# A graph attention phase whose maxima are dealt out three later: seventeen before the first bend, and each head's spread, turn and division three units on

## The chip, the cores and the metric

The kernel runs on one core of one Trainium2 chip. The metric is the time of one execution in microseconds (us), as the median over runs. PE is the matrix engine TensorE, DVE the vector engine, ACT the scalar engine, POOL GpSimd and SP the engine that here only issues DMAs. Every engine works through its own instructions in order and meets the others at semaphores.

## The reference, cut to what matters

A graph of 1250 nodes and 40000 edges goes through a 12-head graph attention with a residual and a layer norm, and then through three relational graph convolutions and a second norm. The change touches the attention alone:

```python
a1 = jnp.einsum('nhd,hd->nh', ft, attn_l)
a2 = jnp.einsum('nhd,hd->nh', ft, attn_r)
e = jax.nn.leaky_relu(a1[src] + a2[dst], negative_slope=NEG_SLOPE)
m = jax.ops.segment_max(e, dst, num_segments=n)
ee = jnp.exp(e - m[dst])
denom = jax.ops.segment_sum(ee, dst, num_segments=n)
alpha = ee / denom[dst]
agg = jax.ops.segment_sum(alpha[:, :, None] * ft[src], dst, num_segments=n)
```

The kernel does it densely: an earlier phase has counted the edges between every pair of nodes into `csum` (1250 x 1250) and has marked the missing ones in `nbr`.

## The kernel before, in words

The attention phase lies between the counting and the convolutions. Its work is cut into units: head h (of 12) and tile s (of 10, 125 nodes each), written (h,s) below, 120 in all, `u = 10 h + s`. For one unit:

- `best(u)` on DVE (line 857): the largest `a1` over the neighbours of each node of the tile, read from `a1`, a row of PSUM spread over all partitions.
- `bend_low(u)` on DVE (869, "bend" below): the first half of the leaky relu, from `r1` (PSUM, the head's lower row spread over all partitions) and `lowb` (SBUF, brought by DMA), into one of five buffers `y`. It waits until POOL has used the buffer: for unit u - 5.
- `bend(u)` and `exponent(u)` on ACT (772, 777): relu, then exponential, the relu of unit u + 1 being issued ahead of the exponential of unit u.
- `weights(u)` on POOL (732): times `csum`, into one of three buffers `pw`. It waits for `gather(u - 3)`.
- `gather(u)` on PE (953): matmuls into the head's sums `po`, in PSUM.

For one head:

- `spread(h)` on PE (919): writes `a1` for the maxima of head h, after all of head h - 1 are taken. Its third piece shares a PSUM bank with `r1`, and waits for a bend.
- `lows(h)` on POOL (705 to 724): eleven small operations that turn the ten maxima of head h into rows; it waits for `maxed` to reach 10 (h + 1), which is all maxima of head h. In POOL's order `lows(h + 2)` stands between `weights(h,9)` and `weights(h+1,0)`.
- `turn_low(h)` on PE (939), then `keep_low(h)` on ACT (782), then DMAs from SP (653, 657, 660) to a row in DRAM and back into `a_rows` and `lowb`.
- `spread_r1(h)` on PE (932): writes `r1` for the bends of head h, issued after `gather(h-1,5)`.
- `keep_sums(h)` on ACT (795), `turn_sums(h)` on PE (961; its result lies where `a1` lies), `divide(h)` on DVE (874 to 879) and `add(h)` on POOL (739) finish the head.

`MAXIMA[s]` lists which tiles of head h + 2 have their maximum taken after the bend of unit (h,s). All twenty maxima of heads 0 and 1 are taken ahead of the first bend. `keep_sums(h-1)` and `keep_low(h+1)` come on ACT after `exponent(h,2)`, and `gather(h,0)` waits for both.

Of the kernel before, what the change touches and what calls it, by code (L numbers as in the profile page):

```python
# [23 lines left out]
T = 125  # L24
NT = N // T
# [554 lines left out]
Y_AT = [(u + 3) % YS for u in range(NU)]  # L580
WIDENED = [6, 7, 8, 9, 0, 1, 2, 3, 4, 5]
GONE = 1e25
MAXIMA = [(), (), (0,), (1,), (2,), (3,), (4, 5), (6,), (7,), (8, 9)]
SPANS = [(0, 512), (512, 512), (1024, N - 1024)]
R1_SPANS = [(286, 512), (798, N - 798), (0, 286)]

# [1 line left out]
def attention(nc, io, dram, stage, x, res, share, oT, cols, csum, csum16, nbr, y, stored, proj_out, rows_out, node, ident):  # L588
# [3 lines left out]
    with ExitStack() as ctx:  # L592
# [99 lines left out]
        def _(pool):  # L692
# [56 lines left out]
                pool.wait_ge(kinds, 4)  # L749

            lows(0)
            lows(1)
            for u in range(NU):
                h, s = divmod(u, NT)
                weights(u)
                if s == NT - 1 and h + 2 < H:
                    lows(h + 2)
                if s == 3 and h >= 2:
                    add(h - 2)
                if s == 5 and h == H - 2:  # L760
                    kinds_and_zeros()
# [5 lines left out]
        @block.scalar  # L767
        def _(act):
            def bend(u):
                h, s = divmod(u, NT)  # L770
                act.wait_ge(zed, u + 1)
                nc.scalar.activation(y[:, Y_AT[u]], y[:, Y_AT[u]], ACT.Relu, scale=-1.0,
                                     bias=a1_low[:, s, h:h + 1]).then_inc(bent, 1)

            def exponent(u):
                act.wait_ge(bent, u + 1)
                nc.scalar.activation(y[:, Y_AT[u]], y[:, Y_AT[u]], ACT.Exp, scale=-1.0).then_inc(raised, 1)

            def keep_low(h):
                act.wait_ge(low_turned, h + 1)  # L780
                act.wait_ge(low_out, 16 * h)
                nc.scalar.copy(row[:], turned_low).then_inc(low_kept, 1)

            def first_low():
                act.wait_ge(low_kept, 1)
                act.dma_start(dram["low"][0].rearrange("m (t p) -> (m t) p", p=T), row[:]).then_inc(low_out, 16)
                act.wait_ge(low_out, 16)
                act.dma_start(a_rows[rows_of(0), :], dram["low"][0, 0:2]).then_inc(r1_in[0], 16)
                act.dma_start(lowb[:, 0], dram["low"][0, 2:3].to_broadcast([T, N])).then_inc(low_in[0], 16)

            def keep_sums(h):
                act.wait_ge(summed, (h + 1) * NT)
                act.wait_ge(low_turned, min(h + 3, H))
                act.wait_ge(o_turned, h)
                nc.scalar.copy(oT, po[:, 0:N].rearrange("p (t n) -> p t n", t=NT)).then_inc(o_kept, 1)

            act.wait_ge(proj_out, 16 * NT)
            for t in WIDENED:
                if t == 0:
                    keep_low(0)  # L800
                    first_low()
                    act.wait_ge(stored[0], 16 * (R + 1) * (NT // 2))
                if t == 3:
                    act.wait_ge(stored[1], 16 * (R + 1) * (NT // 2))
                nc.scalar.copy(csum[:, t], csum16[:, t]).then_inc(widened, 1)
            keep_low(1)
            bend(0)
            for u in range(NU):
                h, s = divmod(u, NT)
                if u + 1 < NU:  # L810
                    bend(u + 1)
                exponent(u)
                if s == 2 and h:
                    keep_sums(h - 1)
                    if h + 1 < H:
                        keep_low(h + 1)
            keep_sums(H - 1)

        @block.vector
        def _(dve):  # L820
# [61 lines left out]
            for t in range(NT):  # L882
                best(t)
            for t in range(NT):
                best(NT + t)
                if t == NT // 2:
                    weight_turned()
            for h in range(H):
                for s in range(NT):
                    bend_low(h * NT + s)  # L890
                    if h >= 2 and s == 1:
                        divide(h - 2)
                    if h == H - 1 and s == 3:
                        degrees()
                    if h + 2 < H:
                        for t in MAXIMA[s]:
                            best((h + 2) * NT + t)
            kind_tables()
            most()
            divide(H - 2)  # L900
# [6 lines left out]
        def _(pe):  # L907
            def spread(h):
                to = a1 if h else r1
                if h >= 2:  # L910
                    pe.wait_ge(maxed, h * NT)
                for i, (o, w) in enumerate(SPANS if h else R1_SPANS):
                    if h == 1 and i == 2:
                        pe.wait_ge(maxed, NT)
                    if h >= 2 and i == 2:
                        pe.wait_ge(zed, (h - 2) * NT + 3)
                    if h >= 4 and i == 0:
                        pe.wait_ge(shared, h - 3)
                    ins = nc.tensor.matmul(to[:, o:o + w], pick[0:A1_K, h:h + 1].to_broadcast([A1_K, T]),  # L919
                                           a_rows[0:A1_K, o:o + w].bitcast(F32R), start=True, stop=True)  # L920
                ins.then_inc(a1_set, 1)

            def spread_r1(h):
# [4 lines left out]
                    pe.wait_ge(maxed, NT)  # L928
                for o, w in R1_SPANS:
                    if o == 0:  # L930
                        pe.wait_ge(maxed, min(h + 2, H) * NT)
                    ins = nc.tensor.matmul(r1[:, o:o + w], pick[at, H:H + 1].to_broadcast([2, T]),
                                           a_rows[at, o:o + w].bitcast(F32R), start=True, stop=True)
                ins.then_inc(r1_set, 1)

            def turn_low(h):
                pe.wait_ge(low_ready, 3 * h + 3)
                pe.wait_ge(low_kept, h)
                nc.tensor.transpose(turned_low, lows_of[:, h % 2].rearrange("p m t -> p (m t)"), ident[0:T, 0:T]).then_inc(low_turned, 1)

            def gather(u):
                h, s = divmod(u, NT)
                pe.wait_ge(weighed, u + 1)
                if s == 0:
# [1 line left out]
                    if h == 0:  # L946
                        pe.wait_ge(ones, 1)
                    pe.wait_ge(o_kept, h)
                    pe.wait_ge(low_kept, min(h + 2, H))
                    if h == 0:  # L950
                        pe.wait_ge(wfc_kept, 2)
                for o, w in SPANS:
                    ins = nc.tensor.matmul(po[:, o:o + w], x[:, s, h], pw[:, u % 3, o:o + w], start=s == 0, stop=s == NT - 1)  # L953
                ins.then_inc(summed, 1)
# [14 lines left out]
            spread(1)  # L969
            turn_low(0)  # L970
            spread_r1(0)
            turn_low(1)
            spread(2)
            for u in range(NU):
                h, s = divmod(u, NT)
                gather(u)
                if s == 5 and h + 1 < H:
                    spread_r1(h + 1)
                    if h >= 1:
                        turn_sums(h - 1)  # L980
                if s == 6 and h + 3 < H:
                    spread(h + 3)
                if s == NT - 1 and h + 2 < H:
                    turn_low(h + 2)
                if s == 5 and h == H - 1:
                    turn_sums(h - 1)
            turn_sums(H - 1)


# [647 lines left out]
```

## Time and profile before

| | |
|---|---|
| median of 3 runs | 2357.75 us (2356.49 to 2358.66) |
| the profiled execution: its time | 2353.26 us |
| its span, first to last instruction | 2351.1 us |
| outside the span | 2.16 us |
| attention phase in the span | 332.8 to 751.4, 418.6 us |
| busy in that phase: PE, DVE, ACT, POOL | 331.0, 369.4, 318.2, 362.2 us |
| mean granted TensorE clock, whole span | 0.969 of full speed |

Times in the profile are microseconds from the start of the span. Over the whole span PE is the busiest engine, but that is the convolutions' doing; the attention phase keeps PE, DVE, ACT and POOL all busy for 76 to 88% of it, and none of them all the time. What sets its length has to be read from who waits for whom in one head.

### The profile page before, as it was taken

What the parts mean: (1) busy time and instruction counts of PE and PEld (TensorE: products, weight loads), DVE (VectorE), ACT (ScalarE), POOL (GpSimd) and SP (SyncE); (2) the same over time, 40 slices, a digit from 0 to 9 for tenths busy, and PEclk for the clock granted to TensorE, in tenths of its full rate; (3) what the DMA queues carried; (4) which work ended last, traced back from release to release, by engine and by line L of the source; (5) the groups of instructions that cost most, each with busy time, mean ns of one, the idle gap of its engine ahead of it and who ended that gap; (6) DMA issues with size and microseconds to landing.
All of it is one profiled execution on the core that took longest, in us unless ns stands there. A gap on an engine that the chain in (4) does not pass through costs nothing.

```text
span 2351.1 us, 29738 instructions
## 1 busy us (share of the span) xinstructions
PE 2151.0 (91%) x10896; PEld 1806.1 (77%) x10897; DVE 1207.6 (51%) x1846; ACT 786.0 (33%) x1071; POOL 515.9 (22%) x565
## 2 busy tenths in 40 slices
PE   4988856888887799999999999999999999999997
PEld 2544532333333799999999999999999899999997
DVE  7887779999977632323323522332322432334335
ACT  1133337888875411212212411211211321212212
POOL 1000016999997100000000100000100100000000
PEclk8999977999998899999999999999999999999998
DMA  1123323111110544334434424333434424345332
GB/s 51 50 93 100 115 94 103 33 34 34 34 36 28 150 136 106 96 87 108 112 90 109 112 73 106 105 96 93 115 98 115 120 71 114 102 115 143 108 93 78
DMA packets 190931, 214.97 MB, mean 91 GB/s; under 512 B 160498, under 2 KB 164057, under 8 KB 190789
## 3 DMA queue, kind: packets, MB, share of 16 engines
q1 hardware_dynamic: 170015, 108.58, 17.4%
q0 software_dynamic: 20032, 102.21, 14.6%
q10 hardware_dynamic: 767, 2.57, 0.3%
q8 instruction: 80, 1.31, 0.2%
q14 instruction: 37, 0.30, 0.0%
HBM read 182.51 MB, written 30.70 MB: 91 GB/s over the span
## 4 chain that ended last, share of the span: by engine, by line
PE 62%; DVE 3%; DMA 2%; ACT 1%; issue 1%; POOL 0%; ACTq 0%; DVEq 0%
PE banks L1218 32%; PE banks L1190 28%; DMA w_raw<-in_L_gnn_w_root_dram 2%; DVE w_lo L1449 1%; ACT w_hi L1324 1%; PE banks L1242 1%; DVE norm_stats L1421 0%; DVE res L1417 0%; PE banks L1260 0%; DVE tail_stats L1500 0%; DVE h_lo L1480 0%; DVE back L1498 0%; ACT accT L1353 0%; DVE g_lo L1471 0%; DVE h_lo L1442 0%
## 5 line engine op out<-in xcount | busy, mean ns | idle before, releaser
L1190 PE MATMUL banks<-ct_in,h_hi 125*128 125x416 f32 (+1 forms) x1710 | 604.4, 353 | 5.0 <-issue 5.0
L1190 PE MATMUL banks<-ct_in,h_lo 125*128 125x416 f32 (+1 forms) x1710 | 603.6, 353 | 0.0
L1218 PE MATMUL banks<-g_hi,w_hi 128*128 128x416 f32 (+1 forms) x1440 | 513.2, 356 | 6.4 <-DVE g_lo L1471 6.3
L1218 PE MATMUL banks<-g_hi,w_lo 128*128 128x416 f32 (+1 forms) x1440 | 511.2, 355 | 0.0
L1218 PE MATMUL banks<-g_lo,w_hi 128*128 128x416 f32 (+1 forms) x1440 | 507.4, 352 | 0.0
L1449 DVE TENSOR_TENSOR w_lo<-w_raw,w_hi 128x768 fp32r<-128x768 f32 (+1 forms) x228 | 227.8, 1000 | 437.8 <-ACT w_hi L1324 437.7
L1157 POOL DMA_DIRECT2D w_raw<-in_L_gnn_w_rel_dram x171 | 92.0, 538 | 1140.6 <-DVE w_lo L1449 1131.4
L1324 ACT CAST w_hi<-w_raw 128x768 fp32r<-128x768 f32 (+1 forms) x228 | 197.9, 868 | 431.4 <-PE banks L1218 360.5
L1340 ACT CAST g_hi<-gs 128x416 fp32r<-128x416 f32 (+3 forms) x180 | 97.4, 541 | 705.9 <-DVE gs L1459 705.9
L1190 PEld LDWEIGHTS banks<-ct_in,h_hi 125*128 125x128 f32 x1710 | 322.9, 189 | 8.7 <-issue 5.4
L1190 PEld LDWEIGHTS banks<-ct_in,h_lo 125*128 125x128 f32 x1710 | 324.0, 189 | 4.2
L953 PE MATMUL head_sums<-pw,x 125*65 125x512 f32 x720 | 276.1, 533 | 45.7 <-POOL pw L732 29.8
L732 POOL TENSOR_TENSOR pw<-y,csum 125x1250 f32<-125x1250 f32 x120 | 313.4, 2649 | 19.2 <-PE head_sums L953 12.1
L1459 DVE TENSOR_TENSOR gs<-banks,inv 128x416 f32<-128x416 f32 (+3 forms) x180 | 106.6, 592 | 395.1 <-PE banks L1190 395.1
L1218 PEld LDWEIGHTS banks<-g_hi,w_hi 128*128 128x128 f32 x1440 | 272.7, 189 | 15.8 <-DVE w_lo L1449 6.2
L1218 PEld LDWEIGHTS banks<-g_hi,w_lo 128*128 128x128 f32 x1440 | 273.4, 190 | 2.3
L1218 PEld LDWEIGHTS banks<-g_lo,w_hi 128*128 128x128 f32 x1440 | 272.1, 189 | 2.7
L953 PEld LDWEIGHTS head_sums<-pw,x 125*65 125x65 f32 x720 | 97.0, 142 | 218.1 <-issue 168.0
L319 DVE TENSOR_SCALAR oh_key<-iota_key,edge_cols,minus_window 125x750 bf16<-125x750 uint16 x480 | 195.1, 475 | 56.1 <-issue 29.2
L869 DVE SCALAR_TENSOR_TENSOR y<-spreads,a_high,low_spread 125x1250 f32<-125x1250 f32 x120 | 180.4, 1514 | 31.1 <-POOL pw L732 18.0
L503 PE MATMUL win<-oh_key,oh_rem 125*128 125x375 bf16 x960 | 179.0, 328 | 12.8 <-issue 9.0
L857 DVE CUSTOM_DVE_ANT_0 junk<-spreads,nbr 125x1250 bf16<-125x1250 f32 x120 | 171.5, 1452 | 13.5 <-PE spreads L919 13.4
(206 smaller groups left out, 1510.8 us busy)
## 6 DMA issues: line engine op xcount, KB each, us to landing
w_raw<-in_L_gnn_w_rel_dram POOLq DMA_DIRECT2D x117, 384.0 KB, 4.3
ct_in<-s_ct SPq DMA_DIRECT2D x72, 610.4 KB
w_raw<-in_L_gnn_w_rel_dram POOLq DMA_DIRECT2D x54, 448.0 KB, 5.9
s_ct<-ct_stage SPq DMA_DIRECT2D x30, 610.4 KB
w_raw<-in_L_gnn_w_root_dram POOLq DMA_DIRECT2D x39, 384.0 KB, 4.4
w_raw<-in_L_gnn_w_root_dram POOLq DMA_DIRECT2D x18, 448.0 KB, 5.9
low_spread<-s_low SPq DMA_DIRECT2D x11, 610.4 KB
x_tile<-in_x_dram POOLq DMA_DIRECT2D x10, 375.0 KB, 9.0
```

Source lines behind the costliest of these rows:

```text
L319: nc.vector.tensor_scalar(oh_key[:, p, b], iota_key[:].rearrange("e s r d -> e (s r d)"), edge[:, 1, bass.ds(c, 1)], minus_w[:, bass.ds(w, ...
L503: ins = nc.tensor.matmul(win[:, p, m, 0:BANK * KEY], oh_rem[:, bass.ds(q + b // 2, 1), :, b % 2].rearrange("e q s -> e (q s)"), oh_key[:, ...
L732: nc.gpsimd.tensor_tensor(pw[:, u % 3], y[:, Y_AT[u]], csum[:, u % NT], ALU.mult).then_inc(weighed, 1)
L857: nc.vector.tensor_tensor_reduce(junk[:, u % 2], a1 if h else r1, nbr[:, t], 1.0, -NOEDGE / 10, ALU.subtract, ALU.max, tops[:, u:u + 1]).t ...
L869: nc.vector.scalar_tensor_tensor(out=y[:, Y_AT[u]], in0=r1, scalar=a1_high[:, s, h:h + 1], in1=lowb[:, h % 2], op0=ALU.add, op1=ALU.max).t ...
L953: ins = nc.tensor.matmul(po[:, o:o + w], x[:, s, h], pw[:, u % 3, o:o + w], start=s == 0, stop=s == NT - 1)
L1190: ins = nc.tensor.matmul(pb[0:rows, PA, 0:s.w], a, b, start=j == 0, stop=j == len(pairs) - 1)
L1218: ins = nc.tensor.matmul(pb[:, m, 0:s.w], a, b, start=s.first and j == 0, stop=s.last and j == len(parts) - 1)
L1324: nc.scalar.copy(w_hi[:, s.wi % WS, 0:s.mt * 128], w_raw[:, s.wi % 2, 0:s.mt * 128]).then_inc(w_hi_done, 1)
L1340: nc.scalar.copy(g_hi[0:rows, s.gi % 2, 0:s.w], gs[0:rows, 0:s.w]).then_inc(g_hi_done, 1)
L1449: nc.vector.tensor_tensor(w_lo[at], w_raw[:, s.wi % 2, 0:s.mt * 128], f32(w_hi[at]), ALU.subtract).then_inc(w_lo_done, 1)
L1459: nc.vector.tensor_tensor(gs[0:rows, 0:s.w], pb[0:rows, PA, 0:s.w], inv[0:rows, s.slab % 2, 0:s.w], ALU.mult).then_inc(gs_done, 1)
```

## The change

Seventeen maxima are taken ahead of the first bend (`LEAD = 17`) and not twenty. The list `MAXIMA` is written in units ahead of (h,0), and is shifted: the last three maxima of head h + 1 now follow the bends of (h,0), (h,1) and (h,2), and head h + 2 starts after the bend of (h,5). With them move: `spread(h + 3)` on PE from behind `gather(h,6)` to behind `gather(h,9)`, its third piece waiting for three bends more; `turn_sums(h - 1)` from behind `gather(h,5)` to behind `gather(h,8)`; `divide(h - 2)` from the bend of (h,1) to that of (h,4). At the start `lows(1)` goes from ahead of `weights(0)` to behind `weights(1)` on POOL, `turn_low(1)` and `spread(2)` from ahead of `gather(0)` to behind `gather(1)` on PE, and `keep_low(1)` from ahead of the first relu to behind `exponent(4)` on ACT. `turn_low(1)`, which now falls into an open sum in the same PSUM bank, is written as a matmul with the identity that doesn't start a sum.

```diff
-MAXIMA = [(), (), (0,), (1,), (2,), (3,), (4, 5), (6,), (7,), (8, 9)]
+LEAD = 17
+MAXIMA = [(17,), (18,), (19,), (), (), (20,), (21,), (22, 23), (24,), (25, 26)]
...
             lows(0)
-            lows(1)
             for u in range(NU):
                 h, s = divmod(u, NT)
                 weights(u)
+                if u == 1:
+                    lows(1)
                 if s == NT - 1 and h + 2 < H:
                     lows(h + 2)
...
-            keep_low(1)
             bend(0)
...
                 exponent(u)
+                if u == 4:
+                    keep_low(1)
...
             for t in range(NT):
-                best(NT + t)
+                if NT + t < LEAD:
+                    best(NT + t)
...
-                    if h >= 2 and s == 1:
+                    if h >= 2 and s == 4:
                         divide(h - 2)
...
-                    if h + 2 < H:
-                        for t in MAXIMA[s]:
-                            best((h + 2) * NT + t)
+                    for t in MAXIMA[s]:
+                        if h * NT + t < NU:
+                            best(h * NT + t)
...
-                        pe.wait_ge(zed, (h - 2) * NT + 3)
+                        pe.wait_ge(zed, (h - 2) * NT + 6)
...
-                        pe.wait_ge(maxed, min(h + 2, H) * NT)
+                        pe.wait_ge(maxed, min(h * NT + LEAD, NU))
...
-                nc.tensor.transpose(turned_low, lows_of[:, h % 2].rearrange("p m t -> p (m t)"), ident[0:T, 0:T]).then_inc(low_turned, 1)
+                low = lows_of[:, h % 2].rearrange("p m t -> p (m t)")
+                if h == 1:
+                    nc.tensor.matmul(turned_low, low, ident[0:T, 0:T], start=False, stop=False,
+                                     skip_group_check=True).then_inc(low_turned, 1)
+                else:
+                    nc.tensor.transpose(turned_low, low, ident[0:T, 0:T]).then_inc(low_turned, 1)
...
-                    pe.wait_ge(low_kept, min(h + 2, H))
+                    pe.wait_ge(low_kept, min(h + 2, H) if h else 1)
...
+                if u == 2:
+                    pe.wait_ge(low_kept, 2)
...
             spread_r1(0)
-            turn_low(1)
-            spread(2)
             for u in range(NU):
                 h, s = divmod(u, NT)
                 gather(u)
+                if u == 1:
+                    turn_low(1)
+                    spread(2)
                 if s == 5 and h + 1 < H:
                     spread_r1(h + 1)
-                    if h >= 1:
-                        turn_sums(h - 1)
-                if s == 6 and h + 3 < H:
+                if s == 8 and h >= 1:
+                    turn_sums(h - 1)
+                if s == NT - 1 and h + 3 < H:
                     spread(h + 3)
                 if s == NT - 1 and h + 2 < H:
                     turn_low(h + 2)
-                if s == 5 and h == H - 1:
-                    turn_sums(h - 1)
             turn_sums(H - 1)
```

## Rows read from the trace of the kernel before

**Rows 1.** Window table, attention: stretch; busy PE, PEld, DVE, ACT, POOL; PEclk, DMA
```profile
332.80:751.40 418.60, 330.96 (x1045) 139.03 (x1045) 369.42 (x409) 318.17 (x275) 362.23 (x272) 0.91 0.14 43
```

**Rows 2.** Timeline of DVE in one head: start, us, operation, [idle before <-releaser]
```profile
517.29 2.95 DVE L869 SCALAR_TENSOR_TENSOR y<-spreads,a_high,low_spread 125x1250 f32<-125x1250 f32 x2 [0.49 <-PE spreads L932]
520.16 0.16 DVE L874 TENSOR_SCALAR den<-spreads 125x10 f32<-125x10 f32 x1
...
521.34 1.51 DVE L869 SCALAR_TENSOR_TENSOR y<-spreads,a_high,low_spread 125x1250 f32<-125x1250 f32 x1
523.31 1.46 DVE L857 CUSTOM_DVE_ANT_0 junk<-spreads,nbr 125x1250 bf16<-125x1250 f32 x1 [0.45 <-PE spreads L919]
...
524.69 1.51 DVE L869 SCALAR_TENSOR_TENSOR y<-spreads,a_high,low_spread 125x1250 f32<-125x1250 f32 x1
526.12 1.45 DVE L857 CUSTOM_DVE_ANT_0 junk<-spreads,nbr 125x1250 bf16<-125x1250 f32 x1
...
547.66 1.52 DVE L869 SCALAR_TENSOR_TENSOR y<-spreads,a_high,low_spread 125x1250 f32<-125x1250 f32 x1 [0.48 <-PE spreads L932]
```

**Rows 3.** Timeline of POOL in the same head
```profile
521.83 2.40 POOL L732 TENSOR_TENSOR pw<-y,csum 125x1250 f32<-125x1250 f32 x1 [0.35 <-PE head_sums L953]
524.19 0.21 POOL L705 TENSOR_TENSOR bias_steps<-tops,a_col 125x10 f32<-125x10 f32 x1
...
526.83 10.38 POOL L732 TENSOR_TENSOR pw<-y,csum 125x1250 f32<-125x1250 f32 x4
537.17 1.55 POOL L739 TENSOR_TENSOR res<-x,res 125x640 f32<-125x640 f32 x1
```

**Rows 4.** Timeline of PE in the same head
```profile
517.18 2.40 PE L961 MATMUL spreads<-wfcT,res 65*125 65x65 f32 x20
519.42 2.27 PE L953 MATMUL head_sums<-pw,x 125*65 125x512 f32 x6
...
522.91 0.36 PE L919 MATMUL spreads<-a_rows,pick_rows 24*125 24x226 f32 x1 [0.57 <-DVE y L869]
...
529.55 0.27 PE L939 MATMUL head_sums<-ident,low_cols 125*30 125x125 f32 x1
531.39 8.58 PE L953 MATMUL head_sums<-pw,x 125*65 125x512 f32 x24 [1.57 <-ACT low_rows L782]
...
544.38 2.32 PE L953 MATMUL head_sums<-pw,x 125*65 125x512 f32 x6 [0.49 <-POOL pw L732]
546.63 0.99 PE L932 MATMUL spreads<-a_rows,pick_rows 2*125 2x512 f32 x3
```

**Rows 5.** Timeline of all engines at the start of the phase
```profile
357.82 0.28 ACTq L789 DMA_DIRECT2D low_spread<-s_low  x1
...
363.58 0.60 PE L932 MATMUL spreads<-a_rows,pick_rows 2*125 2x286 f32 x1 [3.15 <-DVE tops L857]
...
365.81 4.37 DVE L869 SCALAR_TENSOR_TENSOR y<-spreads,a_high,low_spread 125x1250 f32<-125x1250 f32 x3 [2.28 <-issue]
...
371.34 4.76 POOL L732 TENSOR_TENSOR pw<-y,csum 125x1250 f32<-125x1250 f32 x2 [5.06 <-ACT y L777]
...
373.80 13.36 PE L953 MATMUL head_sums<-pw,x 125*65 125x512 f32 x30 [3.01 <-POOL pw L732]
```

**Rows 6.** Timeline of DVE and POOL: the turn to head 1, `lows(2)` and `lows(11)`
```profile
395.39 4.37 DVE L869 SCALAR_TENSOR_TENSOR y<-spreads,a_high,low_spread 125x1250 f32<-125x1250 f32 x3 [0.69 <-PE spreads L932]
...
402.01 0.21 POOL L705 TENSOR_TENSOR bias_steps<-tops,a_col 125x10 f32<-125x10 f32 x1
...
680.27 0.21 POOL L705 TENSOR_TENSOR bias_steps<-tops,a_col 125x10 f32<-125x10 f32 x1
```

**Rows 7.** Window table of PE alone: stretch, busy (x), PEclk (0.50 is half the clock), DMA
```profile
549.80:552.00 2.20, 2.20 (x6) 0.50 0.00 0
```

**Rows 8.** Timeline: a gather at half the clock, and a wait of POOL after one
```profile
395.29 4.20 PE L953 MATMUL head_sums<-pw,x 125*65 125x512 f32 x6
...
553.88 2.40 POOL L732 TENSOR_TENSOR pw<-y,csum 125x1250 f32<-125x1250 f32 x1 [2.02 <-PE head_sums L953]
```

## The prediction

> **What bounds the kernel now.** I read the page first. It makes PE the busiest engine of the span, but the change touches only the attention phase, so I asked the window table for that phase: no engine is busy all the time, and DVE and POOL are nearest to it [rows 1]. A busy share doesn't say what sets the pace there. The timelines of DVE, POOL and PE over one head do, read side by side from one first bend to the next: 517.29 to 547.66, a turn of 30.37 us [rows 2]. What is to be seen is a ring. PE spends 2.40 on turn_sums right behind spread_r1, then makes gather(h,6) (2.27) [rows 4]; POOL's weights(h,9), which needs that gather's buffer, starts just behind it after 0.35 of waiting, and lows follows [rows 3]. lows starts 524.19 - 517.29 = 6.90 after the first bend; from there weights, add, weights, gather(h,5) and spread_r1 lead to the next first bend, 547.66 - 524.19 = 23.47 later. 6.90 + 23.47 = 30.37. DVE loses only 0.49 and 0.45 to PE in the turn [rows 2]. So POOL's own work is 30.37 - 0.35 = 30.02 per head and DVE's 30.37 - 0.94 = 29.43; what can be won by unblocking PE is a third of a microsecond in a quiet head. Some heads are longer: from lows(2) at 402.01 to lows(11) at 680.27 [rows 6] the mean of nine turns is 30.92, because in a few of them PE falls to 1.2 GHz (PEclk 0.50) behind turn_sums [rows 7] and POOL then waits 2.02 [rows 8].
>
> **The change, part by part: the steady head.** Moving turn_sums takes 2.40 out from in front of gather(h,6), so POOL's 0.35 goes. But lows(h+2), which stays behind weights(h,9), needs all maxima of head h + 2. Before, these were done by the end of unit (h,9); now the last three follow the bends of (h+1,0), (h+1,1) and (h+1,2). A bend costs 1.43 before the next operation can start (524.69 to 526.12), a maximum 1.38 (523.31 to 524.69) [rows 2]. Three bends and two maxima are 3 x 1.43 + 2 x 1.38 = 7.05, the third maximum is recorded for 1.46, and I allow 0.1 for the semaphore (a bend that ends at 522.85 starts PE at 522.91 [rows 2, 4]): lows starts 8.6 after the first bend. It started at 6.90, so the turn grows by 1.7, since nothing on the way from lows to the next first bend gets shorter: spread_r1 still stands behind gather(h,5), which before started at 544.38 behind POOL, with spread_r1 at 546.63 behind that [rows 4]. The wait is on POOL, and everything behind it there (weights(h+1,0) and all that follow) waits too.
>
> Second, what that wait does to DVE. The bend of (h+1,5) needs weights(h+1,0) done. lows takes 526.83 - 524.19 = 2.64 and that weights 2.40 [rows 3]: done at 8.6 + 5.04 = 13.7. DVE would be there at 8.43 + 2 x 1.43 + 1.18 for the division (520.16 to 521.34 [rows 2]) = 12.5. DVE idles 1.2. The division is thereby hidden, but DVE has 1.2 + 30.37 = 31.6 in such a turn, still less than the ring, so this costs nothing more.
>
> Third, what the later spread does. Its third piece waits for that bend: 13.7 + 1.51 + 0.06 = 15.3, for 0.36. turn_low, now queued behind it on PE, starts at about 15.7; from a turn_low to gather(h,0) it is 531.39 - 529.55 = 1.84, through keep_sums and keep_low on ACT; a gather takes 8.58 / 4 = 2.15 [rows 4]. gather(h+1,0) is done at 19.75, and weights(h+1,3) needs its buffer: 19.85. By its own pace it would start at 8.6 + (537.17 - 524.19) - 2.36 = 19.2 [rows 3]. So 0.65 more. A turn is 8.6 + 23.47 + 0.65 = 32.7; in head 1, where POOL has no add yet (1.55 [rows 3]), I take 31.2. Bounds: if the two weights behind add ran as fast as a lone one (2.40 against 2.6 on average, 10.38 / 4 [rows 3]) and the 0.65 vanished, a turn would be 31.6, DVE's own; if PE has to run its gathers at half the clock, 4.20 for 2.27 [rows 4, 8], 1.9 more for each one on the ring.
>
> **The start.** Three maxima fewer are 3 x 1.38 = 4.1 less on DVE ahead of the first bend. I cost this at nothing: r1 was ready at 363.58 + 0.60 = 364.18, yet the first bend started at 365.81, so it was waiting for something later than DVE and PE; what fits is the DMA of lowb, issued at 357.82 [rows 5], which the change doesn't touch. The three maxima now stand between the first bends. The second bend ends at 365.81 + 1.43 + 1.38 + 1.51 = 370.13 and not 368.75; weights(0), which came 2.59 behind that at 371.34, comes at 372.7; gather(0) 2.46 later at 375.2 [rows 5]. PE is cold there: 4.2 for that gather [rows 8], some 2.6 for the next, then turn_low(1) and spread(2), 1.1: a1 is ready at 383.1. DVE gets there after six bends and three maxima, 365.81 + 8.58 + 4.14 = 378.5, and idles 4.6. Seven maxima and four bends (15.4) and a wait like the 0.69 before [rows 6] put the first bend of head 1 at 399.2 for 395.39, and lows(2) 8.6 behind it, at 407.8 for 402.01 [rows 6]: 5.8 lost. lows(1), 2.64 on POOL, lies in the time for which POOL then has no bends to work on. keep_low(1) and its DMAs start some 17 us later than before, at about 383.5, and are due at 399.2; the DMA of lowb took at most 365.81 - 357.82 = 8.0 [rows 5], so they are hidden, with 4 to 5 us to spare. turn_low(1) as a matmul is not in this trace; between 0.27 (a transpose [rows 4]) and twice that, once: nothing.
>
> **The sum.** lows(11) comes at 407.8 + 31.2 + 8 x 32.7 = 700.6 for 680.27: + 20.3. Behind lows(11) no maxima or spreads are left but those done, POOL works through as before, and the later turn_sums(10) lies beside weights: nothing. To this comes PE's clock. I reckon with two or three falls more on the ring at 1.9, 5 us, since PE will now wait for the maxima ahead of turn_sums (some 2 us), for the bend inside spread (1.2) and, as before, 1.57 for ACT [rows 4], all close together. Against the profiled execution's 2353.26 (span 2351.1 and 2.16 around it) that is 2378.6; against the median of the runs, 2357.75, it is 2383.
>
> **The rivals.** (1) The other side: POOL falls behind DVE so far that the maxima are always done when it reaches lows, and with turn_sums gone it runs through at 30.02 a head. From lows(2) at 407.8 nine such turns end at 678.0, 2.3 less than now, which is no change; if the start were hidden as well, 8 less: 2350. It decides if POOL reaches lows later than 8.6 behind the first bend. Against it: from lows to the next first bend the path leads over POOL itself, so DVE can't gain on POOL by more than that path allows. (2) The start is lost, but POOL's weights run fast and the turns are DVE's 31.6 (30.1 without add): lows(11) at 407.8 + 30.1 + 8 x 31.6 = 690.7, 10.4 later: 2368. (3) PE's clock falls in every head. Before, PE at half the clock follows turn_sums [rows 7]; the change puts a wait ahead of turn_sums and two behind it. With 1.9 to 3.5 more in each of eight turns, less the 5 already taken: 2393 to 2406. The Trainium skill (TensorE: Matmul & The Clock Gate, Part 1) says that the slow clock is the default and that activity lifts it; by that rule the added idle time speaks for this rival. The trace agrees in so far as a gather behind a long wait took 4.20 and not 2.27 [rows 4, 8]. (4) The change does nothing because the ring is elsewhere: 2357.
>
> **How the numbers follow.** My forecast of 2383 has 0.66, between 2372 and 2394; rival 1 has 0.06 for 2350 and 0.03 for no change; rival 2 0.12; rival 3 0.11; rival 4 0.02. About 0.2% (4.7 us) is what a measurement can tell from no change. Faster 0.07, same 0.05, slower 0.88. The range leaves out rival 1, rival 4 and the ends of 2 and 3: 2367 to 2400.
>
> **What would show it.** In the profile after: the first bend still near 365.8, with DVE idle about 6 ahead of it; a DVE wait of 4 to 5 for spreads in head 0; POOL idle ahead of every lows (L705 released by the maxima, L857); lows 8.6 behind the first bend; a turn of 32 to 33; DVE released by POOL once per head, about 1.2. If POOL shows no wait ahead of lows, or the turn is under 30.4, the prediction is wrong; if the first bend comes 4 us earlier, the start was mis-read.

## The result, and the profile after

The changed kernel takes 2405.1 us (median of 4 runs, 2400.56 to 2407.69) against 2357.12 us for the kernel before on the same chip: a ratio of 1.0205, with a 95% interval of 1.0191 to 1.0218. It is slower by 48 us, where 25 were forecast with a range that ended 42 above. The profiled execution took 2405.09 us for 2353.26, its span 2402.9 for 2351.1, so 51.8 us are to be found in it.

The window table over 320 us inside the attention phase of the kernel after (stretch; busy PE, PEld, DVE, ACT, POOL with counts; PEclk, DMA share, GB/s):

```profile
400.00:720.00 320.00, 273.17 (x773) 107.80 (x774) 269.17 (x300) 231.51 (x201) 266.32 (x198) 0.87 0.13 38
```

The same stretch of the kernel before had 276.38, 289.67, 265.12 and 306.25 us of PE, DVE, ACT and POOL, at 0.97 of the clock. DVE, ACT and POOL all do less in the same time, and PE is nearly as busy for 773 recorded instructions as it was for 891: its work has become slower.

One head, on DVE, in its timeline (start, us, operation, [idle before <-releaser]), which answers to [rows 2]:

```profile
541.53 1.52 DVE L872 SCALAR_TENSOR_TENSOR y<-spreads,a_high,low_spread 125x1250 f32<-125x1250 f32 x1 [1.58 <-PE spreads L936]
...
555.25 1.52 DVE L872 SCALAR_TENSOR_TENSOR y<-spreads,a_high,low_spread 125x1250 f32<-125x1250 f32 x1 [1.17 <-POOL pw L733]
...
576.06 1.52 DVE L872 SCALAR_TENSOR_TENSOR y<-spreads,a_high,low_spread 125x1250 f32<-125x1250 f32 x1 [1.59 <-PE spreads L936]
```

The turn is 576.06 - 541.53 = 34.53 us for 30.37. On POOL, for [rows 3]:

```profile
550.12 0.21 POOL L706 TENSOR_TENSOR bias_steps<-tops,a_col 125x10 f32<-125x10 f32 x1 [1.88 <-DVE tops L860]
...
552.75 7.57 POOL L733 TENSOR_TENSOR pw<-y,csum 125x1250 f32<-125x1250 f32 x3
562.94 2.85 POOL L733 TENSOR_TENSOR pw<-y,csum 125x1250 f32<-125x1250 f32 x1 [2.62 <-PE head_sums L964]
```

POOL waits twice now. First 1.88 ahead of lows, for the last maximum: lows starts 550.12 - 541.53 = 8.59 behind the first bend. Then 2.62 ahead of weights(h+1,3), for gather(h+1,0). The rest of the turn is 576.06 - 550.12 = 25.94, where 23.47 was before [rows 2, 3]. PE, for [rows 4], shows why that gather is late:

```profile
550.14 2.37 PE L972 MATMUL spreads<-wfcT,res 65*125 65x65 f32 x20 [1.89 <-issue]
552.35 3.96 PE L964 MATMUL head_sums<-pw,x 125*65 125x512 f32 x6
556.23 0.96 PE L923 MATMUL spreads<-a_rows,pick_rows 24*125 24x512 f32 x3
557.12 0.28 PE L948 MATMUL head_sums<-ident,low_cols 125*30 125x125 f32 x1
558.98 10.28 PE L964 MATMUL head_sums<-pw,x 125*65 125x512 f32 x24 [1.57 <-ACT low_rows L784]
```

PE waits 1.89 for the maxima as well, since turn_sums writes where they are read (the profile names no releaser for this wait; the kernel lets turn_sums wait for `maxed`, and it starts when the last maximum is done). Behind turn_sums gather(h,9) takes 3.96 and not 2.27. turn_low comes behind the spread at 557.12, then PE waits 1.57 for ACT, and the four gathers behind it take 10.28 and not 8.58. weights(h+1,3) would have been ready at 552.75 + 7.57 = 560.32 and starts at 562.94. The clock, in windows of 2 us over the same stretch:

```profile
549.60:551.60 2.00, 1.46 (x14) 1.49 (x14) 2.00 (x4) 1.67 (x3) 1.31 (x6) 1.00 0.00 0
551.60:553.60 2.00, 2.00 (x11) 1.12 (x11) 1.93 (x4) 2.00 (x2) 1.76 (x7) 0.79 0.00 0
553.60:555.60 2.00, 2.00 (x4) 0.70 (x3) 0.83 (x2) 0.38 (x1) 2.00 (x2) 0.50 0.00 0
...
557.60:559.60 2.00, 0.62 (x2) 0.33 (x3) 2.00 (x3) 2.00 (x3) 2.00 (x1) 1.00 0.00 0
559.60:561.60 2.00, 2.00 (x3) 0.47 (x2) 2.00 (x4) 2.00 (x3) 0.72 (x1) 0.50 0.17 25
561.60:563.60 2.00, 2.00 (x5) 0.84 (x4) 2.00 (x2) 2.00 (x3) 0.66 (x1) 0.65 0.25 100
```

PEclk is 1.00 (2.4 GHz) through turn_sums, 0.50 (1.2 GHz) in gather(h,9), full again around the spread, and 0.50 once more in gather(h+1,0). From head 3 on every turn goes like this. In the turn of head 2 gather(h,9) still took 2.27, behind the same kind of wait (1.91), and the clock fell only with the wait of 1.56 inside the spread. Two of the nine turns are worse (36.6): there the clock is down from turn_sums to turn_low, gather(h+1,0) starts 18.92 behind the first bend and not 17.45, and weights(h+1,3) waits 4.7.

The start, on DVE:

```profile
367.21 1.52 DVE L872 SCALAR_TENSOR_TENSOR y<-spreads,a_high,low_spread 125x1250 f32<-125x1250 f32 x1 [6.91 <-issue]
...
384.83 1.46 DVE L860 CUSTOM_DVE_ANT_0 junk<-spreads,nbr 125x1250 bf16<-125x1250 f32 x1 [4.83 <-PE spreads L923]
400.98 1.52 DVE L872 SCALAR_TENSOR_TENSOR y<-spreads,a_high,low_spread 125x1250 f32<-125x1250 f32 x1 [0.69 <-PE spreads L936]
```

The ledger, in profiled executions. What lies ahead of lows(0) came 0.9 later (349.70 for 348.79). lows(2) starts at 409.56 for 402.01 [rows 6], 7.55 later, so head 0 itself lost 6.6. lows(11) starts at 725.38: the nine turns take 315.8 for 278.3, 37.6 more. From lows(11) to the first operation behind the phase it is 77.8 for 71.1, 6.7 more. 0.9 + 6.6 + 37.6 + 6.7 = 51.8.

### The profile page after: what moved, and what is told of

Same layout as the page of the kernel before. It is cut to its first block, busy times and chain, and to the rows that moved or that the text cites. A ratio compares the mean times of both kernels' runs of the same rounds, so it can differ in the third digit from the quotient of the medians.

```text
span 2402.9 us, 29741 instructions
## 1 busy us (share of the span) xinstructions
PE 2186.7 (91%) x10897; PEld 1815.4 (76%) x10898; DVE 1210.5 (50%) x1846; ACT 785.7 (33%) x1071; POOL 515.7 (21%) x565
## 4 chain that ended last, share of the span: by engine, by line
PE 60%; DVE 2%; DMA 2%; ACT 1%; issue 0%; POOL 0%; ACTq 0%; DVEq 0%
PE banks L1228 32%; PE banks L1200 28%; DMA w_raw<-in_L_gnn_w_root_dram 2%; DVE w_lo L1459 1%; ACT w_hi L1334 1%; PE banks L1252 1%; DVE norm_stats L1431 0%; DVE res L1427 0%; PE banks L1270 0%; DVE h_lo L1490 0%; ACT accT L1363 0%; DVE tail_stats L1510 0%; DVE back L1508 0%; PE banks L1239 0%; DVE g_lo L1481 0%
## 5 line engine op out<-in xcount | busy, mean ns | idle before, releaser
L964 PE MATMUL head_sums<-pw,x 125*65 125x512 f32 x720 | 309.1, 582 | 52.1 <-POOL pw L733 34.3
L964 PEld LDWEIGHTS head_sums<-pw,x 125*65 125x65 f32 x720 | 103.4, 153 | 249.5 <-issue 185.1
L774 ACT ACTIVATE y<-y,a_low 125x1250 f32<-125x1250 f32 x120 | 159.7, 1331 | 70.1 <-DVE y L872 70.0
```

## The experiments

My theory once the trace was read: three causes one behind the other. The three maxima hold lows back by 1.7 a turn (the wait). turn_low stands behind a spread that waits for a bend (the order). And PE's clock falls in its new idle time (the clock). The rivals were that the wait alone explains the turn and the rest only fills it, that the order of PE explains it without the clock, or the clock without the order. "Mean turn" is from the first bend of head 1 to that of head 10, over nine: 30.59 before, 35.09 after. The expectations call the ten experiments e1 to e10, in the order in which they stand here. Ratios are against runs of the kernel before on the same chip; these had medians of 2355.4 to 2357.4, so medians of different experiments can be compared to some 2 us.

**The wait alone, in the kernel before.** Nothing is moved; lows only waits for the fourth bend of the next head.

```diff
                 pool.wait_ge(maxed, (h + 1) * NT)
+                if h >= 2:
+                    pool.wait_ge(zed, (h - 1) * NT + 4)
```

> The kernel before, with one wait more and nothing moved: lows(h) for h of 2 and over also waits until the fourth bend of head h - 1 has been made, which is about 8.9 us behind that head's first bend, where it started 6.9 behind it. The ring theory (first bend, lows, weights, gather(h,5), spread_r1, next first bend) says that every turn grows by about 2.1 us, from 30.9 to 33.0 on average, and the kernel by about 20 us, to 2377, more if TensorE's clock falls more often. The rival, that only the new order on PE costs and POOL has slack for such a wait, says under 2 us.

Measured: 2371.6 us, ratio 1.0069 (1.0048 to 1.0091), mean turn 32.83.

```profile
537.96 0.21 POOL L707 TENSOR_TENSOR bias_steps<-tops,a_col 125x10 f32<-125x10 f32 x1 [2.11 <-issue]
```
```profile
528.92 2.94 DVE L871 SCALAR_TENSOR_TENSOR y<-spreads,a_high,low_spread 125x1250 f32<-125x1250 f32 x2 [2.25 <-PE spreads L934]
...
561.24 2.95 DVE L871 SCALAR_TENSOR_TENSOR y<-spreads,a_high,low_spread 125x1250 f32<-125x1250 f32 x2 [1.27 <-PE spreads L934]
```
```profile
522.02 6.11 PE L955 MATMUL head_sums<-pw,x 125*65 125x512 f32 x12 [2.00 <-POOL pw L734]
```

lows starts 537.96 - 528.92 = 9.04 behind the first bend, and the turn is 561.24 - 528.92 = 32.32: 23.28 behind lows, where 23.47 was before. So in a quiet head lows 2.14 later makes the turn 1.95 longer: a wait ahead of lows is on the ring and costs nearly its length. The mean turn grew by 2.2, but not by the wait alone: in six of the nine turns PE's clock fell as well (33.1 to 33.3 us). In four of these it fell in the gathers of (h,4) and (h,5), 6.11 for two behind a wait of 2.00 for POOL, which with the clock up took 2.31 each behind the same wait. The wait added here also ends 0.45 later behind the first bend than the one of the change, so the third of the loss that this kernel shows (0.0069 of 0.0205) is more than the share of the change's own wait.

**Eighteen maxima.** The changed kernel with two maxima behind the first bends in place of three.

```diff
-LEAD = 17
-MAXIMA = [(17,), (18,), (19,), (), (), (20,), (21,), (22, 23), (24,), (25, 26)]
+LEAD = 18
+MAXIMA = [(18,), (19,), (), (), (), (20, 21), (22,), (23, 24), (25,), (26, 27)]
```

> The changed kernel with eighteen maxima ahead of the first bend and the last two behind the bends of (h,0) and (h,1); spread, turn and division stay three units later. lows should then no longer wait for maxima: they are done 5.8 us behind the first bend, and lows starts at about 6.7 for 8.6. The ring theory: each turn about 1.9 us shorter than in the changed kernel (35.1 on average), so 33.2, and the kernel about 17 us faster than the changed one, 2388; less if the wait on PE for the sixth bend and the half clock behind it come with it. The rival, that the order on PE is all of it: no gain, 2405.

Measured: 2381.22 us, 1.0104 (1.0079 to 1.0129), mean turn 33.07. PE:

```profile
540.31 2.27 PE L964 MATMUL head_sums<-pw,x 125*65 125x512 f32 x6
545.00 0.36 PE L923 MATMUL spreads<-a_rows,pick_rows 24*125 24x226 f32 x1 [1.37 <-DVE y L872]
545.29 0.28 PE L948 MATMUL head_sums<-ident,low_cols 125*30 125x125 f32 x1
547.15 10.22 PE L964 MATMUL head_sums<-pw,x 125*65 125x512 f32 x24 [1.58 <-ACT low_rows L784]
```

One maximum less takes both waits away, that of POOL ahead of lows and that of PE ahead of turn_sums, and gather(h,9) is back at 2.27. Half of the loss is gone. The mean turn is what I expected (33.2), the time 7 us less; half of that lies behind lows(11), where weights(10,3) waits 0.67 for 3.34. But the clock still falls behind the waits of 1.37 and 1.58, in every head, and weights(h+1,3) waits 2.75 in this head and 3.2 to 3.6 in most.

**turn_low ahead of the spread.** The changed kernel with the two steps behind gather(h,9) exchanged.

```diff
+                if s == NT - 1 and h + 2 < H:
+                    turn_low(h + 2)
                 if s == NT - 1 and h + 3 < H:
                     spread(h + 3)
-                if s == NT - 1 and h + 2 < H:
-                    turn_low(h + 2)
```

> The changed kernel with turn_low(h + 2) issued ahead of spread(h + 3) on PE, nothing else. lows still waits for the maxima (8.6 behind the first bend), but turn_low, keep_sums and keep_low no longer wait for the sixth bend, so gather(h,0) comes some 2 us earlier and PE has one gap less. Theory: the wait of weights(h,3) for gather(h,0), 2.6 to 4.7 us in the changed kernel, falls to under 1; turns of about 32.3 for 35.1, the kernel 20 to 25 us faster than the changed one, about 2382. The rival, that the wait of lows for the maxima alone makes the loss: no gain beyond 5 us.

Measured: 2387.95 us, 1.0131 (1.01 to 1.0163), mean turn 33.87. PE:

```profile
545.85 3.80 PE L972 MATMUL spreads<-wfcT,res 65*125 65x65 f32 x20 [1.87 <-issue]
549.43 4.22 PE L964 MATMUL head_sums<-pw,x 125*65 125x512 f32 x6
553.49 0.27 PE L948 MATMUL head_sums<-ident,low_cols 125*30 125x125 f32 x1
553.69 0.82 PE L923 MATMUL spreads<-a_rows,pick_rows 24*125 24x512 f32 x3
555.34 8.58 PE L964 MATMUL head_sums<-pw,x 125*65 125x512 f32 x24 [0.82 <-ACT low_rows L784]
```

ACT copies the rows while PE spreads, so the wait for ACT is 0.82 and gather(h+1,0) runs at 2.4 GHz (PEclk 1.00), in all turns from head 2 to 9 but one (head 3: 11.57 for the four gathers, and POOL waits 3.35). What is left is the fall in turn_sums and gather(h,9), and now these two stand on the way to turn_low. 17 of the 48 us come back, less than I expected.

**PE kept busy.** The changed kernel with matmuls of the identity with itself, six ahead of turn_sums and three ahead of the third piece of the spread, into a stretch of PSUM that nothing reads. The sums are the same.

```diff
+            def warm(n):
+                for _ in range(n):
+                    nc.tensor.matmul(pc[0:T, 1384:1384 + T], ident[0:T, 0:T], ident[0:T, 0:T], start=False, stop=False,
+                                     skip_group_check=True)
...
+                    if h >= 3 and i == 2:
+                        warm(3)
...
                 if s == 8 and h >= 1:
+                    warm(6)
                     turn_sums(h - 1)
```

> The changed kernel with idle matmuls on PE in two of its gaps, into unused columns of the sums' bank: six (125x125, f32) ahead of turn_sums and three ahead of spread's third piece, for every head. They add work and take none away. If the fallen clock is what makes weights(h,3) wait 2.6 to 4.7 us, where I had worked out 0.65, this wait falls to about 0.7 to 1.5, gather(h,9) and gather(h,0) take 2.3 and not 4, turns go to about 32.8 and the kernel to about 2385. If the clock is only a by-product, the time stays at 2405 or grows.

Measured: 2394.58 us, 1.0166 (1.014 to 1.0192), mean turn 34.31, and from head 5 on turns of 33.0 to 33.4 and of 35.1 in alternation. Two heads in a row, first PE, then POOL:

```profile
558.30 8.58 PE L971 MATMUL head_sums<-pw,x 125*65 125x512 f32 x24 [1.58 <-ACT low_rows L784]
...
591.33 11.58 PE L971 MATMUL head_sums<-pw,x 125*65 125x512 f32 x24 [1.58 <-ACT low_rows L784]
```
```profile
560.73 2.86 POOL L733 TENSOR_TENSOR pw<-y,csum 125x1250 f32<-125x1250 f32 x1 [1.10 <-PE head_sums L971]
...
595.88 2.86 POOL L733 TENSOR_TENSOR pw<-y,csum 125x1250 f32<-125x1250 f32 x1 [3.21 <-PE head_sums L971]
```

This is the clearest measurement of the clock's part: the same code, with the same idle time of 1.58 ahead, takes 8.58 with the clock and 11.58 without, and weights(h+1,3) waits 1.10 or 3.21. Up to these gathers everything on PE comes at the same distance behind the first bend in both turns. Where the clock holds the turn is 33.03, within 0.3 of my forecast of 32.7 and 2.06 under the changed kernel's mean of 35.09: that is what the clock costs a mean turn there. The six idle matmuls did what they were for: turn_sums waits 0.58 and not 1.89, and gather(h,9) takes 2.26 in every turn from head 3 on, where the changed kernel has 3.88 to 4.37. So there it was the idle time that brought the clock down. In gather(h+1,0) it stayed up in three of nine turns only, which is why the time missed what I expected.

**The old start.** The changed kernel with everything ahead of head 2's maxima as before: all twenty maxima, `lows(1)`, `keep_low(1)`, `turn_low(1)` and `spread(2)` ahead of the first bend. The core of the edit:

```diff
-                if NT + t < LEAD:
-                    best(NT + t)
+                best(NT + t)
...
-                        if h * NT + t < NU:
+                        if 2 * NT * (h == 0) <= h * NT + t < NU:
...
             lows(0)
+            lows(1)
...
             spread_r1(0)
+            turn_low(1)
+            spread(2)
```

> The changed kernel with the start of the kernel before: all twenty maxima, lows(1), turn_low(1), spread(2) and keep_low(1) ahead of the first bend, and from head 1 on the changed order. If the start cost what its trace shows (lows(2) 6 to 7 us later, since three maxima stand between the first bends and DVE waits 4.8 us for spread(2)), this is 5 to 7 us faster than the changed kernel, about 2399, with turns still near 35. If the start costs nothing, because the loss is taken up by slack behind it, 2405.

Measured: 2395.7 us, 1.017 (1.0142 to 1.0198), mean turn 35.09, as in the changed kernel. The new start has no effect on the turns. The medians differ by 9.4 us of the 48 (the ratios by 8), for 5 to 7 expected; not all of that is the start. From lows(0) to lows(2) the changed kernel takes 59.86, this one 52.63 and the kernel before 53.22: 7.2 for the start. Another 4.0 of the profiled executions' difference lies behind lows(11), where weights(10,3) doesn't wait here and waits 3.34 in the changed kernel.

**Eighteen maxima and turn_low first**, the edits of the second and third experiment together.

> Both single edits at once on the changed kernel: eighteen maxima ahead, and turn_low ahead of spread. lows waits for nothing, and gather(h,0) doesn't wait for the sixth bend. The ring theory: if the two losses are separate links of one ring, both go: turns of 31 to 31.5 for 35.1, the kernel about 33 to 37 us faster than the changed one, 2368 to 2372, and TensorE's clock falls in fewer heads, since PE no longer waits ahead of turn_sums. If the two are one loss seen twice, no better than the better of the two, 2381.

Measured: 2365.76 us, 1.0041 (1.0021 to 1.0061), mean turn 31.10. PE and POOL:

```profile
567.06 0.27 PE L948 MATMUL head_sums<-ident,low_cols 125*30 125x125 f32 x1
569.75 0.36 PE L923 MATMUL spreads<-a_rows,pick_rows 24*125 24x226 f32 x1 [1.16 <-DVE y L872]
570.04 10.30 PE L964 MATMUL head_sums<-pw,x 125*65 125x512 f32 x24
```
```profile
560.69 2.40 POOL L733 TENSOR_TENSOR pw<-y,csum 125x1250 f32<-125x1250 f32 x1 [0.89 <-ACT y L779]
563.05 0.21 POOL L706 TENSOR_TENSOR bias_steps<-tops,a_col 125x10 f32<-125x10 f32 x1
565.67 7.56 POOL L733 TENSOR_TENSOR pw<-y,csum 125x1250 f32<-125x1250 f32 x3
573.42 2.87 POOL L733 TENSOR_TENSOR pw<-y,csum 125x1250 f32<-125x1250 f32 x1 [0.19 <-PE head_sums L964]
```

Of POOL's two waits 0.19 is left in this turn, and 0.89 ahead of weights(h,9), for ACT, is new. The clock still falls here: the gathers take 10.30 in this and the next three turns (heads 6 to 9), and 8.61 in those of heads 2 to 5. But gather(h+1,0) no longer has turn_low and ACT's copy between it and the spread, so even at half the clock it is done almost when POOL wants its buffer. In the turns of heads 7 to 9 POOL waits 0.87 to 1.05 for it, and in the last two of them no longer ahead of weights(h,9). The fall costs nothing: the turns of heads 2 to 5 are 30.88 to 30.90, those of heads 6, 8 and 9 30.89. That is 0.5 above the 30.37 of before; what makes up this 0.5 I haven't followed. Turns and time are slightly better than I expected.

**The best version I could see:** the same with the old start.

> The kernel of e6 with the start of the kernel before. The start should give back 5 to 7 us, so 2362 to 2366 by the theory; it beats the kernel before (2357) only if turns come to under 30.5, near POOL's own 30.0, for which PE would have to stay at full clock. The other view, that with the later turn_sums PE never holds POOL up, says 2350.

Measured: 2357.31 us, 1.0006 (0.9993 to 1.0018), mean turn 31.04: no change that can be measured against the kernel before, and 5 us less than the 2362 I expected at best. The old start is worth 8.5 us here in the medians, and 5.8 from lows(0) to lows(2) (57.40 and 51.61). No kernel of these experiments was faster than the kernel before.

**lows one unit later.** The changed kernel with `lows(h + 1)` behind `weights(h,0)`, so that POOL has work while the maxima are taken.

```diff
-                if s == NT - 1 and h + 2 < H:
-                    lows(h + 2)
+                if s == 0 and h and h + 1 < H:
+                    lows(h + 1)
```

> The changed kernel with lows(h + 1) issued behind weights(h,0) on POOL, and so one unit later: POOL no longer stands idle while the maxima are completed (1.9 us a turn), and the sixth bend no longer waits for lows and a weights (1.2 us). The theory: the third piece of spread comes about 1.2 us earlier, gather(h,0) with it, turns near 33, the kernel about 15 to 20 us faster than the changed one, 2387. If what counts is only when lows is ready for turn_low, no gain, since lows then ends no earlier than before.

Measured: 2404.31 us, 1.0208, and a mean turn of 35.36: nothing gained, and my expectation wrong by 17 us. POOL and PE:

```profile
557.13 2.82 POOL L733 TENSOR_TENSOR pw<-y,csum 125x1250 f32<-125x1250 f32 x1 [1.62 <-PE head_sums L964]
...
564.76 2.86 POOL L733 TENSOR_TENSOR pw<-y,csum 125x1250 f32<-125x1250 f32 x1 [4.80 <-PE head_sums L964]
```
```profile
549.81 3.01 PE L972 MATMUL spreads<-wfcT,res 65*125 65x65 f32 x20 [1.90 <-issue]
552.61 4.38 PE L964 MATMUL head_sums<-pw,x 125*65 125x512 f32 x6
```

POOL doesn't wait ahead of lows (550.47), but the maxima hold PE too: turn_sums waits 1.90 for them, all that follows on PE is as late as in the changed kernel and at half the clock, and POOL gives its gain back ahead of weights(h+1,2) and (h+1,3). The turn shown is one of four long ones (36.2 to 36.7); in a quiet one (34.53) turn_low comes 15.46 behind the first bend, for 15.59 in the changed kernel, and lows is long done, at about 11.9. The maxima reach the ring by two doors, and I had counted one.

**turn_low first, and PE kept busy ahead of turn_sums** (the third experiment's edit and `warm(6)` of the fourth).

> The changed kernel with the lows' transpose issued ahead of the spread (as in e3) and six matmuls of no use ahead of the turning of the sums (as in e4), so that TensorE goes into the turning with work behind it; all outputs are the changed kernel's. If both the queue behind the spread and the clock's fall in the turning make weights(h,3) late, both are gone here, and the clock should stay at 2.4 GHz through gather(h,9) too: weights(h,3) waits 0 to 1 us, a turn of 8.6 + 23.5 to 24 = 32.1 to 32.6 us, about 2374 to 2380 us. If the clock falls in the gap of the lows' copy alone, whatever the turning does, a turn stays at 33 us or more and the time above 2381.

Measured: 2379.35 us, 1.0097 (1.0074 to 1.012), mean turn 32.90. In the middle heads POOL:

```profile
543.93 0.21 POOL L706 TENSOR_TENSOR bias_steps<-tops,a_col 125x10 f32<-125x10 f32 x1 [1.88 <-DVE tops L860]
...
546.57 10.52 POOL L733 TENSOR_TENSOR pw<-y,csum 125x1250 f32<-125x1250 f32 x4
```

The four weights run through without a stop: the second wait is gone, the first stays at 1.88, and these turns are 31.9 to 32.0 (first bends at 503.47, 535.34 and 567.38), 1.5 to 1.7 above the 30.37 of before. That is the price of the three maxima alone. The median lies in what I expected, but in part by luck: the mean turn is above the 32.1 to 32.6 I gave, and the clock didn't stay up through gather(h,9) in every turn (3.6 to 3.7 in those of heads 5, 7 and 9, which cost 0.2: 32.04 for 31.87). The mean is higher because of the first turns (70.2 for those of heads 1 and 2 together) and of two later ones of 32.9, in which gather(h+1,0) was at half the clock (10.30 for 8.58) and POOL waited 0.95.

**Eighteen maxima, and PE kept busy inside the spread** (the second experiment's edit and `warm(3)`).

> The changed kernel with eighteen maxima ahead of the first bend (as in e2) and three matmuls of no use ahead of the third piece of the spread, so that TensorE isn't idle while it waits for the bank of that piece; all outputs are the changed kernel's. In e2 weights(h,3) still waited 3.2 us with no wait ahead of the lows. If that wait is the clock's (gather(h+1,0) at half clock behind two idle stretches), it falls to 1 to 1.5 us and a turn to about 31.2 us: about 2361 to 2366 us. If it is the order alone (the transpose behind the spread's third piece, then the ACT copy), it stays near 3 us and the time near that of e2, 2378 to 2383.

Measured: 2377.49 us, 1.0092 (1.0072 to 1.0113), mean turn 32.58. The mean doesn't tell the clock from the order as I meant it to, since the clock fell in eight of nine turns; the ninth does:

```profile
545.80 0.36 PE L930 MATMUL spreads<-a_rows,pick_rows 24*125 24x226 f32 x1 [0.52 <-DVE y L872]
547.95 10.26 PE L971 MATMUL head_sums<-pw,x 125*65 125x512 f32 x24 [1.58 <-ACT low_rows L784]
...
580.72 8.59 PE L971 MATMUL head_sums<-pw,x 125*65 125x512 f32 x24 [1.58 <-ACT low_rows L784]
```
```profile
583.15 2.87 POOL L733 TENSOR_TENSOR pw<-y,csum 125x1250 f32<-125x1250 f32 x1 [1.10 <-PE head_sums L971]
```

The wait inside the spread has shrunk from 1.37 to 0.52 and the clock falls all the same, behind the wait of 1.58 for ACT; weights(h+1,3) waits 2.0 to 3.4 in eight turns, and these are 32.0 to 33.2 long. So three matmuls between two waits weren't enough to keep it up. But in the turn of head 6 (565.18 to 596.34), with the same waits of 0.52 and 1.58, it held: the gathers took 8.59, weights(6,3) waited 1.10 and the turn was 31.16, which is what I had expected if the wait of 3.2 is the clock's. So in this order the clock is worth about 1.6 a turn (31.16 against 32.76 in the turn before), and the 1.10 that is left is the order's.

## Why the prediction was too low

**The ring and its 8.6 us: right.** lows starts 8.59 behind the first bend, DVE waits 1.17 for 1.2, POOL 1.88. The first experiment shows that such a wait costs nearly its length; the ninth that three maxima behind the first bends make a turn of 31.9 to 32.0, 1.6 more, where I had added 1.7.

**The start: right in its mechanism, 0.8 short.** Taking fewer maxima ahead of the first bend gained nothing: DVE idled 6.91 ahead of it. DVE waited 4.83 for the spread (4.6 forecast), and head 0 lost 6.6 (5.8 forecast). The fifth and seventh experiment find 9.4 and 8.5 us in medians, of which 7.2 and 5.8 lie between lows(0) and lows(2).

**The step that failed: the 0.65 for weights(h+1,3), and the 5 us for PE's clock beside it.** I let gather(h+1,0) end at 17.54 + 2.15 + 0.06 behind the first bend. It started on time, at 558.98 - 541.53 = 17.45, but took some 3.9, being at 1.2 GHz, and POOL waited 2.62. I had written down the three idle stretches of PE (about 2, 1.2 and 1.57) and then priced them as two or three falls in the phase; there was one at gather(h+1,0) in every turn, and one at gather(h,9) in seven of the nine. The first of these is the one on the ring in a quiet head. By the fourth experiment the term itself was 1.10 and not 0.65, and the clock adds 1.5 to it in a quiet head (2.62) and 2.1 in the mean turn. The 0.65 was too small by a reading: I had let weights(h+1,3) take 2.36, the length of a lone one, but it takes 2.85 and so starts earlier. Its row in POOL's timeline before:

```profile
534.36 2.85 POOL L732 TENSOR_TENSOR pw<-y,csum 125x1250 f32<-125x1250 f32 x1
```

In the kernel before it starts 534.36 - 524.19 = 10.17 behind lows, so by its own pace at 8.6 + 10.17 = 18.8 behind the first bend and not 19.2 (measured: 560.32 - 541.53 = 18.79), and the term comes to 19.85 - 18.77 = 1.08. The mean turn of 35.09 stands against 32.5 in my sum, or 33.1 with the 5 us, so nine turns were 18 us short: some 3.5 of them by that reading, the rest in the main by the clock. This is rival 3, to which I gave 0.11 and 2393 to 2406. The Trainium skill's rule (TensorE: Matmul & The Clock Gate, Part 1), that the slow clock is the default and activity lifts it, spoke for it. The trace agrees in the main: the gathers behind the new idle stretches ran at PEclk 0.50, and took 3.96 for 2.27. But the rule alone doesn't say in which turn: in that of head 2 gather(h,9) took 2.27 behind 1.91 of idle time.

**The order and the clock.** Undoing the order alone gave 17 us, one maximum less 24, and both together 39. These medians don't price the clock, since the order makes the idle time behind which the clock falls, and it also decides whether a fall counts: in the sixth experiment it came and cost nothing. Turns in which the clock held do price it: 30.37 before, 31.87 with the three maxima behind the first bends (ninth), 33.03 with the order as well (fourth), and 35.09 in the changed kernel's mean. So a turn pays about 1.5 for the wait, 1.2 for the order and 2.1 for the clock. The two in the middle are single turns of kernels with idle matmuls in them, so this is good to a few tenths.

**The tail: wrong, 6.7 for nothing.** I had said that POOL works through as before behind lows(11). But weights(10,3) waits 3.34 there as in any head, which is 3.5 with the rest; in head 11 weights wait twice for gathers, 0.62 and 0.93; and turn_sums(10), which I placed beside weights, stands ahead of the last gather on PE: the last weights is done at 775.07 + 17.28 = 792.35, and its gather starts at 793.76, 1.4 later.

```profile
739.02 2.85 POOL L733 TENSOR_TENSOR pw<-y,csum 125x1250 f32<-125x1250 f32 x1 [3.34 <-PE head_sums L964]
...
775.07 17.28 POOL L733 TENSOR_TENSOR pw<-y,csum 125x1250 f32<-125x1250 f32 x6
```
```profile
791.63 2.29 PE L972 MATMUL spreads<-wfcT,res 65*125 65x65 f32 x20
793.76 2.26 PE L964 MATMUL head_sums<-pw,x 125*65 125x512 f32 x6
```

Closed up: 2378.6 forecast for the profiled execution, 1.8 for lows(2) at 409.56 in place of 407.8 (0.9 of it from ahead of the phase), 18 in the turns and 6.7 behind them are 2405.1, and 2405.09 was measured.

What stays open is why the clock held in some heads and fell in others with the same order and the same idle time, as in the first, fourth and tenth experiment. So I can say what a fall costs here, but not forecast in which head it comes.

## What to carry to other kernels

When a change adds a wait to a ring, look on every other engine for instructions that wait for the same event: here PE's turn_sums stood behind the same maxima as POOL's lows, and relieving POOL alone gained nothing. When several short waits of PE come close together in every turn, take the fall of its clock as a cost of every turn until a row shows otherwise. And let the step that another engine has to answer (turn_low, for ACT's copy) go ahead of a step that fills the time of the answer.

## What the runs showed of the hardware that I had not expected

Short waits were enough to bring the clock down, but not every one did. In the kernel before the wait of 1.57 for ACT stands ahead of gather(h+1,0) too, and the four gathers behind it took 8.58 in the quiet heads [rows 4]. In the changed kernel the same 1.57, with a wait of 1.89 and a turn_sums of 2.37 some 9 us ahead of it, was followed by PEclk 0.50 and 10.26 or more in every head. Behind 1.89 and turn_sums PEclk fell to 0.50 in seven of eight turns, in five of them back at 1.00 before turn_low. With 0.82 or less in place of 1.57 (turn_low first) the four gathers took 8.58 to 8.59 in all turns from head 2 to 9 but one, and in that one the wait was the shortest, 0.26. In the first experiment a single wait of 2.00 was followed by two gathers in 6.11 in four heads, and by 2.31 for each in head 5. Nor is a mean clock a measure of the loss: from 400 to 720 us it was 0.94 in the seventh experiment and 0.97 in the kernel before, at the same total time, since a fall counts only where a gather stands on the ring.
